# Sharing the last exponential of a unit between VectorE and ScalarE, and moving the sums over wavelengths to TensorE

## The reference

```python
Q, K, V = proj(Wq, bq), proj(Wk, bk), proj(Wv, bv)      # 16 heads of 8 features
def wl_step(acc, wl):                                    # 16 wavelengths
    cpm, iw = wl                                         # cos of a phase for each head, a weight
    m = cpm[None, :, None, None]
    scores = jnp.einsum('bhqd,bhkd->bhqk', Q * m, K * m) * SCALE
    scores = scores * jnp.cos(KERR * scores * scores)
    attn = jax.nn.softmax(scores, axis=-1)
    return acc + jnp.einsum('bhqk,bhkd->bhqd', attn, V) * iw, None
combined = acc / 16
out = x + combined @ Wo + bo + experts(xn)
```

## Time and profile before

| | |
|---|---|
| median of three runs | 1883.58 us (1883.06 to 1883.99) |
| the profiled execution | 1883.32 us, its span 1881.6 us |
| ScalarE busy | 97% |
| TensorE busy | 73% |
| VectorE busy | 41% |
| GpSimd busy | 24% |
| granted TensorE clock, mean | 0.987 of full |

### The profile page before, as it was taken

The page is one execution under the profiler, slowest core; times in us unless marked ns, Lnnn a source line. Parts: engine busy times, 40 slices in busy tenths (PEclk is TensorE's granted clock), DMA queues, the critical chain, the costliest instruction groups (busy, mean ns, idle before and its releaser), DMA issues. The chain is left out here.

```text
span 1881.6 us, 42847 instructions
## 1 busy us (share of the span) xinstructions
PE 1381.2 (73%) x18990; PEld 836.5 (44%) x18990; DVE 774.9 (41%) x1452; ACT 1818.4 (97%) x553; POOL 458.9 (24%) x513
## 2 busy tenths in 40 slices
PE   4787787676688888888886667767667676666765
PEld 2354454443455555555554444444344444444444
DVE  7445564333345444444433334333333333333222
ACT  3799999999999999999999999999999999999995
POOL 6222233232122122112122245433212112212111
PEclk8799999999999999999999999999999999999998
DMA  6000110000201111101000000000000000000001
GB/s 203 16 14 15 57 37 31 26 20 14 50 7 38 41 41 41 41 10 33 21 21 14 20 23 13 23 24 16 14 14 2 14 14 14 14 14 2 7 13 30
DMA packets 44985, 49.89 MB, mean 27 GB/s; under 512 B 6725, under 2 KB 37359, under 8 KB 44799
## 3 DMA queue, kind: packets, MB, share of 16 engines
q1 hardware_dynamic: 42463, 42.91, 7.5%
q0 software_dynamic: 2048, 4.20, 0.8%
q10 hardware_dynamic: 288, 0.00, 0.0%
HBM read 30.96 MB, written 15.73 MB: 25 GB/s over the span
## 5 line engine op out<-in xcount | busy, mean ns | idle before, releaser
L933 ACT ACTIVATE Pr<-T 128x4096 f32<-128x4096 f32 x512 | 1796.2, 3636 | 1.3 <-DVE T L852 0.8
L894 PE MATMUL bank<-Pr,Vst 128*32 128x256 f32 x16384 | 992.5, 382 | 429.7 <-ACT Pr L933 264.5
L894 PEld LDWEIGHTS bank<-Pr,Vst 128*32 128x32 f32 x16384 | 575.1, 109 | 752.7 <-issue 569.4
L852 DVE COPY T<-bank 128x512 f32<-128x512 f32 x252 | 174.1, 691 | 482.4 <-PE bank L846 482.2
L939 POOL TENSOR_TENSOR gain<-rsum,iw_s 128x128 f32<-128x128 f32 x63 | 25.3, 402 | 1139.0 <-DVE rsum L925 1139.0
L836 DVE TENSOR_REDUCE negmax<-bank 128x2 f32<-128x512 f32 x256 | 165.0, 686 | 195.3 <-PE bank L830 194.8
L903 DVE COPY pv_s<-bank 128x512 f32<-128x512 f32 x192 | 131.3, 684 | 182.8 <-PE bank L894 182.7
L920 DVE COPY OT<-bank 128x432 f32<-128x432 f32 (+1 forms) x192 | 105.9, 552 | 118.4 <-PE bank L909 118.3
L909 PE MATMUL bank<-ident,pv_s 128*128 128x128 f32 x768 | 118.7, 277 | 24.3 <-DVE pv_s L903 24.3
L948 POOL TENSOR_TENSOR terms<-terms 128x512 f32<-128x512 f32 x126 | 128.1, 1017 | 9.9
L943 POOL TENSOR_TENSOR terms<-OT,gain 128x1024 f32<-128x1024 f32 x63 | 124.6, 1977 | 5.0
(11 more groups left out here) (168 smaller groups left out, 465.1 us busy)
## 6 DMA issues: line engine op xcount, KB each, us to landing
Ks<-qk_parts SPq DMA_DIRECT2D x31, 288.0 KB
Qs<-qk_parts SPq DMA_DIRECT2D x93, 96.0 KB
work<-in_L_ffn_w_dram SPq DMA_DIRECT2D x16, 256.0 KB, 3.9
qk_parts<-Pr SPq DMA_DIRECT2D x8, 384.0 KB, 2.8
qk_parts<-work SPq DMA_DIRECT2D x8, 384.0 KB, 3.1
dispatched<-T SPq DMA_DIRECT2D x5, 512.0 KB, 4.7
region<-dispatched SPq DMA_DIRECT2D x8, 320.0 KB, 3.9
expert_out<-work SPq DMA_DIRECT2D x8, 320.0 KB, 2.8
```

The costliest lines, as they stand in the source:

```text
L852: nc.vector.tensor_copy(T[par][:, ds(p * BANK, BANK)], sc_bank[rr][:, :]).then_inc(sc_read, 1)
L894: ins = nc.tensor.matmul(bank[VC * j:VC * (j + 1), half * SEQ:(half + 1) * SEQ], Vst[par][:, at:at + VC], Pr[rr][:, blk * SEQ:(blk + 1) * ...
L933: nc.scalar.activation(Pr[rr][:, :], T[par][:, :], ACT.Exp, scale=scales[u % 2][w]).then_inc(exp_done, 1)
```

## The change

1. **The last exponential is shared.** In the 28 units from 4 on (`D_UNITS`), wavelength 15 is computed in two parts. ScalarE takes one block of 256 columns in each of four groups of 1024 (`Pr_short`, 1024 columns); VectorE takes the other 3 x 1024 columns (`dve_d_exp`), each chunk of 1024 in seven operations: scale and clamp to an integer (op 0), cut out the mantissa (1) and the exponent (2), and four steps that evaluate a product of two quadratics of the mantissa (3 to 6). `D_OPS_AT` tells how many of the 21 stand in each step: 2, 1, 2, 0, 2, 2, 1, 2, 0, 2, 2, 0, 3, 2, 0, 0. TensorE waits for the three chunks and for ScalarE's part before the matmuls that read them.
2. **Buffers.** The two `Pr` buffers alternate over the whole exponentials alone; `Pr_short` and the three `d_out` have their own place.
3. **Sums.** `OT` and GpSimd's `sum_half` are gone. VectorE works on the turned group in PSUM: reciprocal of the row sums, times the weight, times the values, into `terms`. TensorE adds the wavelengths up with a matmul by the identity for each (`pe_sum`), and VectorE copies the unit's sum to `heads` in step 1 of the next unit (`dve_heads`). The sum of group q is issued two steps after its last wavelength (`SUM_AT`: steps 4, 7, 9, 12, 15, and 0 of the next unit).
4. **The turned maxima** are taken at the end of step 4 (`MAX_AT`) in place of step 11. They and the sums lie in one PSUM bank, `bank_b`: the first sum of a unit waits until VectorE has copied the maxima (`nm_copied`), and the turn of the maxima waits for the copy of the previous unit's sum (`summed`).
5. In the setup GpSimd computes one more small table, `cd`; several buffers have moved.

```diff
-                        nc.gpsimd.tensor_tensor(c_side, scaled, cosine, ALU.mult)
+                        ins = nc.gpsimd.tensor_tensor(c_side, scaled, cosine, ALU.mult)
+                    link(ins)
+                    nc.gpsimd.tensor_scalar(cd[:, :], cw[:, :].rearrange("p (u w) -> p u w", w=W)[:, :, W - 1], LOG2E * MANT, None, ALU.mult)
...
+            def dve_d_exp(dve, u, par, i):
+                c, op = divmod(i, DOPS)
...
+                if op == 0:
...
+                    ins = nc.vector.tensor_scalar(d_scaled[:, :].rearrange("p (j k) -> p j k", k=SEQ), src, cd[:, u:u + 1], FLOOR, ALU.mult, ALU.max)
+                elif op == 1:
+                    dve.wait_ge(d_step, made + 1)
+                    ins = nc.vector.tensor_scalar(d_mantissa[:, :].bitcast(i32), d_scaled[:, :], 0x007FFFFF, 0x3F800000,
+                                                  ALU.bitwise_and, ALU.bitwise_or)
+                elif op == 2:
+                    ins = nc.vector.tensor_scalar(d_scaled[:, :], d_scaled[:, :], 0x40000000, 0x7F800000,
+                                                  ALU.bitwise_xor, ALU.bitwise_and)
+                elif op == 3:
+                    dve.wait_ge(d_step, made + 2)
+                    ins = nc.vector.scalar_tensor_tensor(out_[:, :], d_mantissa[:, :], r1, d_mantissa[:, :], ALU.add, ALU.mult)
+                elif op == 4:
+                    ins = nc.vector.scalar_tensor_tensor(d_mantissa[:, :], d_mantissa[:, :], r2, d_mantissa[:, :], ALU.add, ALU.mult)
+                elif op == 5:
+                    dve.wait_ge(d_step, made + 4)
+                    ins = nc.vector.scalar_tensor_tensor(out_[:, :], out_[:, :], s1, d_scaled[:, :].bitcast(f32), ALU.add, ALU.mult)
+                else:
+                    dve.wait_ge(d_step, made + 6)
+                    ins = nc.vector.scalar_tensor_tensor(out_[:, :], d_mantissa[:, :], s2, out_[:, :], ALU.add, ALU.mult)
...
+                dve.wait_ge(turned, n + 1 + 2)
+                nc.vector.reciprocal(rsum[:, 0:size, :].unsqueeze(3), slots[:, :, :, HD:OC]).then_inc(inverted, 1)
+                dve.wait_ge(inverted, n + 1)
+                nc.vector.tensor_tensor(gain[:, 0:size, :], rsum[:, 0:size, :], weight, ALU.mult).then_inc(gain_ready, 1)
+                dve.wait_ge(gain_ready, n + 1)
...
+                nc.vector.tensor_tensor(terms[n % 2][:, 0:size, :].rearrange("p s (a d) -> p s a d", d=HD), slots[:, :, :, 0:HD],
+                                        gain[:, 0:size, :].unsqueeze(3).to_broadcast([P, size, OTW, HD]), ALU.mult).then_inc(terms_ready, 1)
+
+            def pe_sum(pe, u, q):
+                n = u * GROUPS + q
+                pe.wait_ge(terms_ready, n + 1)
+                if q == 0:
+                    pe.wait_ge(nm_copied, min(u + 2 if u else 1, UNITS - 1) + 2)
...
+                for w in range(FIRST_OF[q], LAST_OF[q] + 1):
+                    ins = nc.tensor.matmul(sum_bank, ident[:, :], terms[n % 2][:, w - FIRST_OF[q], :], start=w == 0, stop=w == W - 1)
+                ins.then_inc(terms_summed, 1)
...
+                if w == W - 1 and u in D_UNITS:
+                    act.wait_ge(pv_done, 2 + u * W)
+                    blocks = T[par][:, :].rearrange("p (j b) -> p j b", j=GR)[:, :, DCHUNKS * SEQ:]
+                    nc.scalar.activation(Pr_short[:, :, :], blocks, ACT.Exp, bias=LN_FACTOR if DCHUNKS % QT else 0.0, scale=scales[u % 2][w]).then_inc(exp_done, 1)
+                    return
...
+            SUM_AT = {last + 2: q for q, last in enumerate(LAST_OF) if last + 2 < W}
...
+            MAX_AT = 4
...
+            D_OPS_AT = (2, 1, 2, 0, 2, 2, 1, 2, 0, 2, 2, 0, 3, 2, 0, 0)
```

More of the change, by code:

```diff
@@ L71, in attention_and_experts @@
     RING = 2
+    DCOLS = 4 * SEQ
+    DCHUNKS = 3
+    SHORT = (COLS // DCOLS - DCHUNKS) * SEQ
+    DOPS = 7
+    MANT = 2.0**23
+    LOG2E = float(np.log2(np.e))
+    FLOOR = -127.0 * MANT
+    QUAD = (-2.20121121, 14.14633, 2.04406053, 2.66350)
+    LN_FACTOR = float(np.log(2.0 * 73.88484))
     ZCOLS = 1024
@@ L131, in attention_and_experts @@
         pv_s = [sb(f"pv_s{i}", [P, BANK]) for i in range(2)]
-        OT = [sb(f"OT{i}", [P, WH * OTW * OC]) for i in range(2)]
-        rsum = [sb(f"rsum{i}", [P, WH * OTW]) for i in range(2)]
-        gain = sb("gain", [P, WH * OTW])
-        terms = sb("terms", [P, WH + 1, OTW * HD])
-        flat_terms = terms[:, :, :].rearrange("p w a -> p (w a)")
-        mv = flat_terms[:, 0:2 * TILES].rearrange("p (t s) -> p t s", s=2)
-        ln = flat_terms[:, 2 * TILES:8 * TILES].rearrange("p (a t) -> p a t", a=6)
+        Pr_short = sb("Pr_short", [P, GR, SHORT])
+        d_scaled = sb("d_scaled", [P, DCOLS], i32)
+        d_mantissa = sb("d_mantissa", [P, DCOLS])
+        d_out = [sb(f"d_out{i}", [P, DCOLS]) for i in range(DCHUNKS)]
+        rsum = sb("rsum", [P, SLOTS, OTW])
+        gain = sb("gain", [P, SLOTS, OTW])
+        terms = [sb(f"terms{i}", [P, SLOTS, OTW * HD]) for i in range(2)]
+        mv = sb("mv", [P, TILES, 2])
+        ln = sb("ln", [P, 6, TILES])
         negmax = [sb(f"negmax{i}", [P, SIDE_TILES]) for i in range(2)]
@@ L998, in attention_and_experts, with whole_before, buffer_of, scores_read @@
                      + [PLAIN] * (LAST - EPAIR - E // 2) + [FINAL])
+            D_UNITS = [u for u in range(UNITS) if KINDS[u // 2] not in (FIRST, SECOND)]
+            WHOLE = [u * W + w for u in range(UNITS) for w in range(W - (u in D_UNITS))]
+            D_OPS_AT = (2, 1, 2, 0, 2, 2, 1, 2, 0, 2, 2, 0, 3, 2, 0, 0)
+            D_DONE = tuple(sum(D_OPS_AT[:w]) for w in range(W + 1))
+            def whole_before(u):
+                return u * W - sum(v < u for v in D_UNITS)
+            def buffer_of(u, w):
+                return (whole_before(u) + w) % 2
+            def scores_read(u):
+                if u == UNITS - 1:
+                    return pair_no(u, 0) - SIDE_B + 2
+                return pair_no(u, 0) + 2
             def units(unit):
@@ L1048, in step @@
                             pe_turn(pe, u, TURN_AT[w])
-                    def after(phase):
-                        if phase == (C if first else B) and two:
-                            pe_turn_max(pe, u + 2)
-                    run_steps(step, after, first)
+                        if w == MAX_AT and two and not first:
+                            pe_turn_max(pe, u + 2, u)
+                        if w in SUM_AT:
+                            pe_sum(pe, u, SUM_AT[w])
+                    run_steps(step, lambda phase: None, first)
                 units(unit)
+                pe_sum(pe, UNITS - 1, GROUPS - 1)
             def plain_vector(dve):
@@ L1080, in step @@
                             dve_products(dve, u, TURN_AT[w])
+                        if w == 1 and u:
+                            dve_heads(dve, u - 1)
+                        if w == 2 and u == 1:
+                            dve_turn_max(dve, 1, 0)
                         if phase == A and two:
@@ L1086, in step @@
                             dve_transposed(dve, pair_no(u, 1, two), 1 - par, k, rr)
+                        if u in D_UNITS:
+                            for i in range(D_DONE[w], D_DONE[w + 1]):
+                                dve_d_exp(dve, u, par, i)
                         if kind == FIRST:
@@ L1096, in step @@
                             dve_turned(dve, u, TURN_AT[w])
+                        if w == MAX_AT and two and not first:
+                            dve_turn_max(dve, pair + 1, par)
                     def after(phase):
@@ L1117, in plain_scalar @@
             def plain_scalar(act):
-                nc.scalar.activation(gain[:, 0:1], one_col[:, :], ACT.Exp).then_inc(exp_table, 1)
+                nc.scalar.activation(gain[:, 0, 0:1], one_col[:, :], ACT.Exp).then_inc(exp_table, 1)
                 for q in range(0, SIDE_B, 2):
@@ L1151, in plain_gpsimd, with unit @@
                     stage_v(pool, u, u)
-                def unit(u, par, last=False):
-                    for half in range(1 if last else 2):
-                        sum_half(pool, nc.gpsimd, pool_step, HALF_STEPS * (2 * u + half), u, half)
+                def unit(u):
+                    for half in range(2):
                         paced = u * W + WH * half + 10
@@ L1166, in plain_gpsimd @@
                 CU = EU + E + 1
-                for u in range(H):
-                    unit(u, u % 2)
+                for u in range(2 * LAST):
+                    unit(u)
                     stage_next(pool, u)
-                for u in range(H, 2 * LAST):
-                    unit(u, u % 2)
-                    stage_v(pool, u + 2, u % 2)
-                unit(UNITS - 2, 0)
-                unit(UNITS - 1, 1, last=True)
             def stage_next(pool, u):
```

126 lines of the change are left out of this document (64 added, 62 removed).

## The result

The changed kernel takes 1964.86 us (median of 4 runs, 1961.46 to 1969.79) against 1883.45 (1883.06 to 1883.99): ratio 1.0434, 95% interval 1.0411 to 1.0457. I had said slower, but 1899 us with a range up to 1942. The profiled run took 1969.79 us, its span 1968.1.

The account below looks back on a forecast made before the run. ScalarE's work bounds the kernel, 97% busy. From 1883.3 us: -72.5 - 1.5 + 10.3 + 11.4 + 33.1 + 26.8 + 2.2 + 0.8 + 5 = +15.6, so 1899 us, range 1882 to 1942.

Parts of the forecast that it names:

- the two places of waiting: ScalarE idle, put down to TensorE, before exponential 2 (0.5, or 1.4 after an expert) and exponential 7 (1.8 or 3.4).
- The short exponential: ScalarE's last exponential in 28 units: 1024 columns take 1.05 us, 0.92 start to start, saving 72.5 us in all.
- The end of the kernel: Last unit, from the end of exponential 14 to the heads: 8.0 us instead of 12.1, gaining 1.5 beyond the exponential.
- (a): VectorE's added one-tensor operations run a column a cycle, at 1.23 us instead of 0.70: 1941 us; chance 0.12.
- (b): The wait at step 4 is hidden, the rest as forecast: 1837 us, faster; chance 0.13.
- the term of the fifth step: P(5), queued behind group 0's sum, waits for VectorE's copy of the maxima: 33.1 plain, 26.8 expert, 2.2 units 1 to 3.
- Shared reads: VectorE and GpSimd operations lock each other out for a whole instruction: 0 to 18 us, taken as 5.
- The boundary: Between units, TensorE's extra small matmuls delay exponential 2: 0.54 us 19 times (10.3), 1.43 behind expert units 8 times (11.4).
- rival (c): TensorE's matmul blocks take their single durations: 0.6 us more at 27 boundaries, 0.2 at each fifth step: 1920; chance 0.10.
- the setup: One more GpSimd operation at the end of its chain before the first exponential: 0.8 us.
- an expert unit loses and a plain one is level: Per unit, 2.59 us saved against 0.54 + 1.84 lost in plain ones and 1.43 + 3.35 with an expert, 2.2 longer.

Follow-up runs that it names:

- the sums alone: Changed kernel with all 512 exponentials whole on ScalarE again, the sums still on TensorE and the maxima turned at step 4: 1884.9 us.
- Experiments 3: Changed kernel plus twelve identity matmuls that nobody reads, filling TensorE's wait in step 4 of the 18 plain units: 1940.7 us.
- experiment 4: Changed kernel plus identity matmuls that nobody reads in TensorE's step 4 wait, 12 in plain units and 14 in units with an expert: 1921.2 us.
- experiment 1: Changed kernel with the sum of group 0 issued in step 5, behind P(5), instead of step 4: 1858.3 us.

## Why the prediction was wrong

**What held.** ScalarE as the bound, the two places of waiting, and the durations. The short exponential takes 1.04 us (1.05 said), the one-tensor operations 0.68 to 0.74 (0.70), the scalar-tensor-tensor ones 1.22 to 1.27 (1.23), the reciprocal 0.45, the terms 0.56. From a short exponential to the next one it is 0.94 us (0.92), so the short ones save 72 us (72.5). ScalarE's busy time of 1753.8 is the 1818.4 of before, less these 72, plus 0.10 for each of 62 breaks, to about 1 us. The end of the kernel, from the end of exponential 14 to the heads, takes 8.1 us (8.0); what comes behind the heads takes 14.6 instead of 13.9, which I had not counted. The first exponential starts 0.6 later (0.8). Rivals (a) and (b) are out. The masks on integers (0.68 to 0.69) and the scalar read per partition (0.74) do run at nearly twice the pace of the two-tensor form (1.22). That was the rule of the Trainium skill's page quoted in the prediction (VectorE: DVE Perf Modes, the perf-mode tier table), which has it for float32; the trace agrees, and shows it for integers too.

**The step that failed is the term of the fifth step**, 33.1 + 26.8 + 2.2 = 62.1 us. It measured 109.0 idle, and 111.7 from start to start. The wait itself was right: at full clock it is 1.73 and 3.25, and 18 x 1.73 + 8 x 3.25 + 2.4 (units 1 to 3, as the sums alone have them) = 59.5 idle, where I had 58. The other 49.5 us are TensorE's clock, but for 0.4. I took the sum and P(5) at 0.67 and 1.93, their durations in rows in which TensorE had come out of short idle times, and put them behind an idle time of 2.9 to 3.4 us that the change itself makes. No rival and no end of the range lets anything run at the half clock. Experiments 3 and 4 keep TensorE at work and take the idle time at step 7 from 109.0 to 63.2 (44 us by the medians). The 3.6 left over the 59.5 can be read in the traces: 3.3 are units 1 and 3, whose sum and P(5) run slow in the kernel of experiment 4 (P(5) 3.14 and 3.03 us) and at full pace with the sums alone (1.93), and 0.4 is unit 7, where VectorE is later and TensorE waits 3.27 instead of 2.90.

**Shared reads**, taken at 5 of 0 to 18: 16.6 idle, 17.0 from start to start. The mechanism and the four units were named. The place was not: I had set the delay against the 1.8 us of slack of turn 2, in step 8, but it was the sum of group 1, ahead of P(8), that waited. The price was taken as one operation of GpSimd. The three ran in a row and the short product of VectorE sat out two, and this wait also brought the clock down.

**The boundary**, 10.3 + 11.4 = 21.7: 25.7 idle without unit 0, 28.4 from start to start. In a plain unit 0.60 + 0.10 = 0.70 against 0.54. In the kernel of experiment 1, from the end of exponential 14 (1400.08) to exponential 2 (1408.64), it is 8.56 and I had 8.34: the turn up to the products is 0.58 instead of 0.44, the sum 0.76 instead of 0.67: these blocks run together less with the block behind them than those of the earlier trace rows did. So rival (c) holds for a third of its price. In the expert units 1.6 to 1.9 of idle time and the 0.10 stand against 1.43; I didn't take that apart.

With these three put right, 1898.9 + 49.6 + 12.0 + 6.7 = 1967, and the profiled run took 1969.8. The other 2.6 are small: the short exponentials save 0.7 less, the end of the kernel 0.9 less, the setup costs 0.3 less, and exponentials in a row follow each other at 3.511 us where it was 3.508. The clock alone carries the time out of the range: the median of 1964.9 less 49 is 1916. The forecast that an expert unit loses and a plain one is level turned into both losing.

## What to carry to other kernels

Before a wait is put ahead of dense work on TensorE, count the work behind it at the half clock as well; a short consumer whose result nobody needs at once (here a sum of 0.8 us) belongs behind the critical products, not ahead of them. When two engines share a buffer or bank, look at who is queued behind the waiting instruction: moving one such instruction by one step was worth 107 us here. And when work moves onto an engine with idle time, the total of that time (VectorE was 41% busy before) says nothing; the longest row of work ahead of each of its hand-overs does.
